# Scoring a softmax attention twice, by query and by key, in place of transposing its probabilities

## The reference, cut to what matters

```python
qh = q.reshape(B, h, dq, Lq)          # h = 8, dq = 16, Lq = 256
kh = k.reshape(B, h, dq, Lk)
vh = v.reshape(B, h, dv, Lk)
qk = jnp.einsum('bhdq,bhdl->bhql', qh, kh) * scale     # scale = 1/4
sm = jax.nn.softmax(qk, axis=-1)
ret = jnp.einsum('bhql,bhdl->bhdq', sm, vh)
x = x + jnp.tanh(g_xattn[3]) * gamma * ret.reshape(B, Dv, Lq)
```

## Time and profile before

| | |
|---|---|
| median of 3 runs | 2673.7 us (2672.37 to 2678.76) |
| the profiled execution | 2675.16 us, of which 2673.4 us are its span |
| PE busy with matmuls, share of the span | 2277.1 us, 85% |
| DVE busy | 1862.6 us, 70% |
| ACT busy | 1348.8 us, 50% |
| POOL busy | 1201.7 us, 45% |
| mean granted TensorE clock | 0.932 of full speed |
| `l3_attention`, first score matmul to last block of values | 2411.22 us to 2632.98 us after the start |

### The profile page before, as it was taken

The page is one execution under the profiler, slowest core; times in us unless marked ns, Lnnn a source line. Parts: engine busy times, 40 slices in busy tenths (PEclk is TensorE's granted clock), DMA queues, the critical chain, the costliest instruction groups (busy, mean ns, idle before and its releaser), DMA issues. The chain is left out here.

```text
span 2673.4 us, 47944 instructions
## 1 busy us (share of the span) xinstructions
PE 2277.1 (85%) x16842; PEld 1948.3 (73%) x16842; DVE 1862.6 (70%) x3807; ACT 1348.8 (50%) x3391; POOL 1201.7 (45%) x1633
## 2 busy tenths in 40 slices
PE   5879993788899968999997699996999994658997
PEld 2368883788888868898987588885888883336775
DVE  5855556698888777878787477775555555975776
ACT  2123332677777757777775233331444442435663
POOL 5800113777888777777776111110344442221112
PEclk9989996799999989999999699997999997767998
DMA  3200001100000011000000300001000000001000
GB/s 129 64 32 1 1 1 55 66 13 15 13 13 17 17 54 31 17 15 15 16 7 1 114 24 25 24 13 54 7 7 7 7 3 1 1 26 35 22 22 33
DMA packets 36925, 68.00 MB, mean 25 GB/s; under 512 B 5713, under 2 KB 25489, under 8 KB 34193
## 3 DMA queue, kind: packets, MB, share of 16 engines
q1 hardware_dynamic: 36688, 64.94, 7.5%
HBM read 58.63 MB, written 6.29 MB: 24 GB/s over the span
## 5 line engine op out<-in xcount | busy, mean ns | idle before, releaser
L1197 PE MATMUL bank<-l_wr,l_xq 128*128 128x128 f32 (+1 forms) x2048 | 280.5, 292 | 19.9 <-POOL l_wxr L1553 9.3
L1197 PEld LDWEIGHTS bank<-l_wr,l_xq 128*128 128x128 f32 x2048 | 257.1, 200 | 21.8 <-issue 15.2
L1315 ACT ACTIVATE xn_T<-bank,l_head_b,l_head_w 128x256 f32<-128x256 f32 x256 | 144.6, 565 | 218.1 <-PE bank L1244 218.1
L1575 POOL TENSOR_TENSOR l_cat<-l_yo,l_eo 128x512 fp32r<-128x512 bf16 x128 | 221.2, 1728 | 57.6 <-DVE l_yo L1398 57.6
L790 PE MATMUL bank<-m_xr,m_wgr 128*128 128x512 f32 x864 | 210.9, 394 | 9.2 <-POOL m_wgr L850 9.2
L1449 DVE TENSOR_REDUCE l_rowsum<-xn_T 128x4 f32<-128x512 f32 x128 | 87.8, 686 | 162.0 <-ACT xn_T L1287 160.4
L1568 POOL TENSOR_TENSOR xn_T<-xn_T,l_rowsum 128x512 f32<-128x512 f32 x128 | 143.1, 1118 | 107.0 <-DVE l_rowsum L1490 107.0
L790 PEld LDWEIGHTS bank<-m_xr,m_wgr 128*128 128x128 f32 x864 | 158.9, 190 | 39.3 <-issue 9.2
L1521 POOL TENSOR_TENSOR l_tiny<-l_tiny,l_minus_half 128x6 f32<-128x6 f32 x128 | 172.3, 1346 | 10.7
L1244 PE MATMUL bank<-ident,l_raw 128*128 128x128 f32 x768 | 113.1, 284 | 73.3 <-DVE l_raw L1455 72.2
L1233 PE MATMUL bank<-l_wpr,l_cat 128*128 128x256 f32 x1024 | 166.1, 305 | 1.9 <-POOL l_cat L1575 1.9
(11 more groups left out here) (323 smaller groups left out, 6339.3 us busy)
## 6 DMA issues: line engine op xcount, KB each, us to landing
l_stage<-in_l_w SPq DMA_DIRECT2D x8, 1024.0 KB, 4.9
m_unsplit<-in_m_w SPq DMA_DIRECT2D x14, 384.0 KB, 3.3
m_wg<-in_m_gu SPq DMA_DIRECT2D x18, 256.0 KB, 2.7
x_norm<-in_ctxT_b SPq DMA_DIRECT2D x32, 128.0 KB, 2.0
l_stage<-in_l_wp SPq DMA_DIRECT2D x4, 1024.0 KB, 4.8
l_saved<-l_xs SPq DMA_DIRECT2D x16, 256.0 KB, 2.0
l_xs<-l_saved SPq DMA_DIRECT2D x16, 256.0 KB, 2.6
l2f_w<-in_l_w SPq DMA_DIRECT2D x3, 1024.0 KB, 7.6
```

What stands on the lines that cost most here:

```text
L1197: e.matmul(bank[:, to:to + width], XQ[:, q % 2, v, k, :], WR[:, j, part, k, at:at + width], start=k == 0 and part == 0, stop=k == KT - 1 a ...
L1315: e.activation(tok(QT[:, n % 2, 3 * x:3 * x + 2, :]), ps[:, 0:2 * P], ACT.Identity, bias=head_b[:, 2 * x:2 * x + 1], scale=head_w[:, 2 * x ...
L1575: e.tensor_tensor(tok(CAT[:, n % 2, :, :]), YO[:, n % 2, :], EO[:, :], ALU.subtract).then_inc(s_cat.sem, 1)
```

## The change

The scores are computed twice. The first time they are laid out by query, as before, and only their maxima are taken. The second time they are laid out by key (keys on the partitions, queries along the free axis), with the maximum of each query already subtracted: the negated maxima are transposed into rows and added into a row of the queries that belongs to the other head and is zero, and the keys hold a row of ones there. ACT then takes the exponent of a whole bank without a bias and writes it where `values` reads it. The transposes of the probabilities, their copies and the buffer `PR` are gone.

In each step now:

- `score(n, half)`: as before, but both halves use the same two banks, so `score(n, 1)` waits for `maximum(n, 0)` and `score(n+1, 0)` for `maximum(n, 1)`.
- `maximum(n, half)`: the same reductions; they write to two columns of a zeroed 128 x 256 tile.
- `turn_maxima(n)`: two 128 x 128 transposes of that tile.
- `add_maxima(n)`: DVE adds them to the masked queries, 128 x 256, giving `XM`.
- `score_by_key(n)`: 16 matmuls (32 rows of keys x 128 keys, against 128 queries), four pairs to four banks.
- ACT: four exponents of 128 x 512.
- `values(n)`: the same matmuls, into one bank `pacc` in place of two.
- `divide(n)`: DVE's reciprocal and multiplication; the addition into `X` is now GpSimd's, and the statistics stand two steps later in DVE's order.

The keys are loaded in two versions (256 KB in place of 128 KB for a batch). DVE zeroes the tile of the maxima once (128 x 512) at the stage's start.

```diff
-            CK = sb(scratch, "l3_ck", [P, 2, D])
+            XM = sb(scratch, "l3_xm", [P, 2, 2, P])
+            CK = sb(scratch, "l3_ck", [P, 2, 2, D])
-            negmax = sb(scratch, "l3_negmax", [P, 2, HEADS])
-            PR = sb(scratch, "l3_pr", [P, 2, HEADS, D])
-            PT = sb(scratch, "l3_pt", [P, 2, KT, HEADS, P])
+            negmax = sb(scratch, "l3_negmax", [P, 2, 2 * P])
+            PT = sb(scratch, "l3_pt", [P, 2, PAIRS, 2, KT, P])
...
-            scores, turned, pacc = banks[0:4], banks[4:6], banks[6:8]
+            scores, by_key, rows_bank, pacc = banks[0:2], banks[2:6], banks[6], banks[7]
...
             def score(e, n, half):
-                if n >= 1:
-                    e.wait_ge(*s_exp(2 * n - 1 + half))
+                if 2 * n + half >= 1:
+                    e.wait_ge(*s_max(2 * n + half))
...
+            def turn_maxima(e, n):
+                e.wait_ge(*s_max(2 * n + 2))
+                if n >= 1:
+                    e.wait_ge(*s_xm(n))
+                for o in range(2):
+                    r = e.transpose(rows_bank[:, o * P:(o + 1) * P], negmax[:, n % 2, o * P:(o + 1) * P], ident[:, :])
+                r.then_inc(s_row.sem, 1)
+
+            def score_by_key(e, n):
+                b = n // 2
+                e.wait_ge(*s_xm(n + 1))
+                if n >= 1:
+                    e.wait_ge(*s_exp(PAIRS * n))
+                for o in range(2):
+                    for k in range(KT):
+                        for p in range(PAIRS):
+                            rows = slice(32 * p, 32 * p + 32)
+                            at = (KT * o + k) * P
+                            r = e.matmul(by_key[p][:, at:at + P], CK[rows, b % 2, o, k * P:(k + 1) * P], XM[rows, n % 2, o, :],
+                                         start=True, stop=True)
+                r.then_inc(s_st.sem, 1)
...
             def tensor(e):
                 begin(e, ends)
                 score(e, 0, 0)
+                score(e, 0, 1)
+                turn_maxima(e, 0)
+                for n in range(N + 1):
+                    if n + 1 < N:
+                        score(e, n + 1, 0)
+                    if n < N:
+                        score_by_key(e, n)
+                    if n + 1 < N:
+                        score(e, n + 1, 1)
+                    if n >= 1:
+                        values(e, n - 1)
+                    if n + 1 < N:
+                        turn_maxima(e, n + 1)
...
             def scalar(e):
                 begin(e, ends)
+                for n in range(N):
+                    e.wait_ge(*s_st(n + 1))
+                    if n >= 2:
+                        e.wait_ge(*s_pv(n - 1))
+                    for p in range(PAIRS):
+                        e.activation(PT[:, n % 2, p, :, :, :].rearrange("p o k t -> p (o k t)"), by_key[p][:, :],
+                                     ACT.Exp).then_inc(s_exp.sem, 1)
...
+            def add_maxima(e, n):
+                e.wait_ge(*s_row(n + 1))
+                if n >= 2:
+                    e.wait_ge(*s_st(n - 1))
+                e.tensor_tensor(XM[:, n % 2, :, :], rows_bank[:, 0:2 * P].rearrange("p (o q) -> p o q", o=2),
+                                XQ[:, n // 2 % 2, :, n % 2 * P:(n % 2 + 1) * P], ALU.add).then_inc(s_xm.sem, 1)
...
             def vector(e):
                 begin(e, ends)
+                dve_own.did(e.memset(negmax[:, :, :], 0.0))
...
+                maximum(e, 0, 0)
+                maximum(e, 0, 1)
+                add_maxima(e, 0)
+                for n in range(N + 3):
+                    if n + 1 < N:
+                        maximum(e, n + 1, 0)
+                        maximum(e, n + 1, 1)
+                        add_maxima(e, n + 1)
+                    if 1 <= n <= N:
+                        divide(e, n - 1)
+                    if n % 2 == 1 and n // 2 + 2 < B:
+                        normalise(e, n // 2 + 2)
+                    if n >= 4 and n % 2 == 0:
+                        b = n // 2 - 2
+                        e.wait_ge(*s_xadd(2 * b + 2))
+                        e.bn_stats(stats[:, b, :], X[:, b, :]).then_inc(bn.sem, 1)
...
             def gpsimd(e):
                 begin(e, ends)
+                separate(e, 0)
                 for s in range(N + 2):
+                    if s % 2 == 0 and s // 2 + 1 < B:
+                        separate(e, s // 2 + 1)
                     if s >= 2:
+                        n = s - 2
+                        b, cols = n // 2, slice(n % 2 * P, (n % 2 + 1) * P)
+                        e.wait_ge(*s_mix(n + 1))
+                        e.tensor_tensor(X[:, b, cols], X[:, b, cols], mixed[:, n % 2, :], ALU.add).then_inc(s_xadd.sem, 1)
```

More of the change, by code:

```diff
@@ L2202, in score @@
                         rows = slice(32 * p, 32 * p + 32)
-                        r = e.matmul(scores[p][:, o * D:(o + 1) * D], XQ[rows, b % 2, o, qt * P:(qt + 1) * P],
-                                     CK[rows, b % 2, :], start=True, stop=True)
+                        r = e.matmul(scores[p % 2][:, o * D:(o + 1) * D], XQ[rows, b % 2, o, qt * P:(qt + 1) * P],
+                                     CK[rows, b % 2, o, :], start=True, stop=True)
                 r.then_inc(s_score.sem, 1)
[L2207 to L2216, removed]
@@ L2229, in values @@
+            def values(e, n):
+                b = n // 2
+                e.wait_ge(*s_exp(PAIRS * n + PAIRS))
+                e.wait_ge(*s_cv(b + 1))
+                if n >= 1:
+                    e.wait_ge(*s_mix(n))
+                for o in range(2):
+                    for k in range(KT):
+                        for at, weights in ((0, CV), (P, colm)):
                             for p in range(PAIRS):
@@ L2289, in maximum, with divide @@
                 if n >= 2:
[L2290 removed]
+                    e.wait_ge(*s_row(n - 1))
                 for p in (2 * half, 2 * half + 1):
[L2292 removed]
+                    r = e.tensor_reduce(negmax[:, n % 2, 32 * p + 16:32 * p + 129:112], scores[p % 2][:, :].rearrange("p (o k) -> p o k", o=2),
                                         AXX, ALU.max, negate=True)
                 r.then_inc(s_max.sem, 1)
[L2296 to L2298 removed]
+            def add_maxima(e, n):
[4 more added lines that the diff above has]
+                                XQ[:, n // 2 % 2, :, n % 2 * P:(n % 2 + 1) * P], ALU.add).then_inc(s_xm.sem, 1)
+            def divide(e, n):
                 e.wait_ge(*s_pv(n + 1))
[L2300 removed]
+                e.reciprocal(rinv[:, n % 2, :], pacc[:, P:2 * P]).then_inc(s_inv.sem, 1)
                 e.wait_ge(*s_inv(n + 1))
@@ L2323, in vector @@
                 e.wait_ge(*gamma(1))
[L2324 to L2336, removed]
+                e.wait_ge(*dve_own.all())
@@ new lines, in separate @@
+            def separate(e, b):
+                e.wait_ge(*s_xn(b + 1))
+                if b >= 2:
+                    e.wait_ge(*s_xm(2 * (b - 1)))
+                for o in range(2):
+                    r = e.tensor_scalar(XQ[:, b % 2, o, :], xn[:, b % 2, :], even[:, o:o + 1], 0.25, ALU.mult, ALU.mult)
+                r.then_inc(s_xq.sem, 1)
+                e.wait_ge(*s_ct(b + 1))
+                if b >= 2:
+                    e.wait_ge(*s_pv(2 * (b - 1)))
+                for o in range(2):
+                    r = e.tensor_tensor(CV[:, b % 2, o, :, :], CT[:, b % 2, :, :], bc(colm[:, o, :], 1, KT), ALU.mult)
+                r.then_inc(s_cv.sem, 1)
```

49 lines of the change are left out of this document (16 added, 33 removed).

## The result

The changed kernel takes 2685.88 us (median of 10 runs, 2683.15 to 2695.85), the kernel before 2674.59 us (10 runs): ratio 1.0048, 95% interval 1.0035 to 1.0061. It is slower by some 11 to 13 us, half a per cent. I had forecast 2677 us and "no change"; the time lies in the stated range (2666 to 2706), but outside the likeliest case's own range (2672 to 2682) and beyond the 8 us that I had called "no change".

What follows compares the result with a forecast made beforehand. PE bounded the stage before; afterwards a PE-DVE loop of 6.75 us would. 27.6 + 28 x 6.75 + 7.5 = 224.1 us (+2.3), plus 0.3 and 0.6, gives +3.2 us: forecast 2677 us, range 2666 to 2706.

Steps and rivals of the forecast that it cites:

- no change: Whole kernel: a time within 0.3%, 8 us, of the kernel before; chance 0.54.
- likeliest case: Stage loop of 6.75 us, give or take 0.15: 2677 us, 2672 to 2682; chance 0.54.
- the step: One loop over PE and DVE in the stage: 6.75 us, against 6.50 before.
- the prediction's own signs: Marks in the new trace, such as 6.75 us steps and PE holes; clock under 1.0 behind 2440 means forecast wrong.
- the clock: Rival: PE's granted clock falls, 3.85 us more a step there, 27 us for seven steps, 2704 us; chance 0.12.
- the rival with the dearer loop: Stage loop of 7.05 us through PE's tiling changes or a slower addition: 8.4 us more, 2685 us; chance 0.16.
- bounds of 6.45 and 7.05: Loop limits: 6.45 us with cheap crossings and free tiling changes, 7.05 with dearer tiling change and addition.
- PE's load: PE's work in the stage: 5.31 us a step, idle 1.44 us ahead of each score(n, 1).
- The serial loads: Rival: score_by_key's loads go one by one, 3.84 us, loop 8.19 us, 40 us more, 2717 us; chance 0.06.
- The rows that spoke against it: Earlier trace, 1430 to 1460 us: PE busy 20.27 of 30 us, a 2.50 us hole, clock kept 1.00.
- Start and end: Stage edges: first values at 21.1 us, score(3, 1) at 27.6, last values 7.5 us behind score(31, 1).
- the forecast for the stage: First score to last values: 27.6 + 28 x 6.75 + 7.5 = 224.1 us, against 221.8 before.

Runs made afterwards that it cites:

- e1: Changed kernel plus five unread float32 128 x 128 matmuls a step behind score_by_key, in PE's hole; 2683.2 us, ratio 1.0023 to the kernel before.
- e4: Changed kernel plus one unread 128 x 256 addition on DVE a step, behind add_maxima; 2743.42 us, ratio 1.0255 to the kernel before.
- e7: e4 plus six unread 128 x 128 matmuls a step behind score_by_key; 2693.62 us, ratio 1.0065 to the kernel before.
- e2: Changed kernel with DVE's divide moved between the maxima of half 0 and half 1; 2665.78 us, ratio 0.9957 to the kernel before.
- e5: e2 with a second bank for the values, turn_maxima writing into the first bank by key; 2655.72 us, ratio 0.9925 to the kernel before.
- e3: Changed kernel with score_by_key's matmuls ordered one partition group after the other; 2699.38 us, ratio 1.0082 to the kernel before.
- e12: e1 run once more, unaltered, beside e11 on one chip; 2681.69 us, ratio 1.0016 to the kernel before.
- e11: Changed kernel run once more, unaltered, beside e12 on one chip; 2688.51 us, ratio 1.0041 to the kernel before.
- e8: Changed kernel with eight filler matmuls on 32 rows a step in the place of e1's five; 2685.56 us, ratio 1.0027 to the kernel before.

## Why the prediction was right, and where it was off

What was right is the step and its mechanism. What failed, by the prediction's own signs, is the clock: stretches under 1.0 behind 2440 were to mean that the forecast is wrong, and two steps at the lower clock that its rival decides; there were eight such steps. The time, 2685.9 us, is within 1 us of the rival with the dearer loop (2685), and that is chance: the loop was not dearer.

- **What bounds the stage.** The step was forecast at 6.75 us and is 6.76. Its parts are where the sum has them: crossings, values ahead of `turn_maxima`, the addition and the division between the halves. In the step shown above no part is off by more than 0.03 us; that they cancel to 0.01 is luck, with bounds of 6.45 and 7.05. e1 shows it from PE's side (1.2 us more work, no time), e4 and e7 from DVE's (0.34 us more work, 0.34 us more time), e2 and e5 by taking 1.27 us out of the loop (6.12 and 5.93 us; 5.88 was worked out). GpSimd is no rival, as shown above.
- **PE's load.** A hole of 1.42 to 1.43 us ahead of `score(n, 1)`, ended by the maxima, was forecast at 1.44. PE is busy 62.89 of 80 us, 5.3 us a step, as forecast. The other signs came too: DVE's hole before the addition (0.96 us), ACT idle 4.70 us of 6.76, its four exponents 2.06 us (2.26 forecast).
- **The serial loads.** Four groups at once do run together (30 instructions in 1.21 us). The price of the rival was wrong: 0.08 us an instruction and not 0.12, so even in turn the block just fits the hole (e3).
- **The clock.** This is the term that was mis-sized: the likeliest case had the clock held throughout, with 0.12 for its fall. Both profiles of the changed kernel have stretches at the lower clock. In the first, the eight longer steps add 2 x (31.5 - 27.1) = 8.8 us. The rival had the number of steps nearly right (a quarter, 7) and the price of one wrong: it doubled all of PE's work, 3.85 us, and measured are 1.1 us, because the clock was down for a part of every second step only. In the chain the scores, values and transposes there take 1.99, 3.57 and 0.63 us in place of 1.13, 1.9 and 0.38. The rows that spoke against it came from full 128-row matmuls with a hole of 2.50 us and a clock of 1.00; here a hole of 1.43 us was enough at times, and holes of 1.80 and 1.40 us in turn (e4) in every step. That the lower clock makes the long steps is seen in them: their blocks of values take up to 3.57 us in place of 1.9. That the hole lets it fall is shown by e1, e7 and e12, where the hole is filled and they are gone, and by the times of e11 and e12, whose intervals don't overlap. That a hole is the only way isn't so: e3 has none.
- **Start and end.** First values 20.9 us after the first score (21.1 forecast). The first block of values took 3.54 us and not 2.72, since the clock rose later in it (0.50 from 2431 to 2434 us, and 0.64 before): 0.8 us. The last block of values comes 7.7 us after the thirtieth, 1.2 us more than worked out: with one bank, `values(31)` waits for the division of 30, which the sum had forgotten. Two steps of the loop without statistics or `normalise` are 6.44 us, 0.6 less together. The first keys took 2.65 us to land (2.6 forecast).

Against the forecast for the stage, 224.1 us, 234.6 were measured: 8.8 of the clock, 0.8 of the first values, 1.2 of the last, less 0.6 of the two short steps, and 28 x 0.01 of the loop. That is 10.5 us, and leaves nothing. Outside the stage 0.9 us more were forecast (first keys, last addition), and 0.5 less were measured.

So PE lost 2.22 us of transposes a step and took on 1.30 us of new work, and the 0.92 us saved went into a wait. The code says why PE and DVE alternate: with the scores in two banks in place of four, each half waits for the maxima of the one ahead. No run gives the scores four banks again, so that these two banks alone make the wait is argued and not shown. The work saved is real: e5, which only puts DVE's division and one bank elsewhere, is 20 us faster than the kernel before.

## What to carry to other kernels

When a change frees the engine that bounds a stage, walk each engine's written order once around and add up what stands between two crossings; here this sum, and no busy share, gave the step, and every part of it to 0.03 us. A buffer given up (two banks of scores for four) may cost as much as the instructions saved, and work that has no place in the loop (the division) should stand in the hole the loop leaves. A hole in TensorE's work isn't free even off the path: it can cost the clock. Matmuls that nobody reads got most of that back here (e1, e12); work that shortened the loop got far more (e2, e5).

## What the runs showed of the hardware

- The clock fell with holes of 1.43 us in each step of 6.76, at places that differ between two executions of one program, and in every step with holes of 1.80 and 1.40 us in turn (e4). It stayed at 1.00 where PE had at most 0.23 us of idle time a step (e1, e7, e8, e12) and with one hole of 0.59 us a step (e5, 2447 to 2610 us).
- In e3 it fell, mean 0.77 in 22 us, while PE was busy 22.00 of 22.00 us. Its instructions use 32 of the 128 rows for much of the step. e8 has such instructions too and kept the clock in its profile. What tells the two apart stays open.
- Float32 matmuls of 32 rows x 128 columns against 128 columns: 32 instructions took 2.71 us one group after the other and 1.21 us (30 of them) with four groups in turn, at the full clock.
